# Layer 0 scan: the backward directions' chunk sums leave PSUM by ScalarE and are added to the kept sums by GpSimd

## Chip, cores and metric

One core of a Trainium2 chip runs the whole program. The metric is the device time of one execution in microseconds (us); lower is better.

## What is computed

The program is a network of four layers on an image batch of 4 x 48 x 48 x 128. The change touches the first layer alone, a selective scan over each image in four directions, cut here to what matters:

```python
# per image: d = 256 channels, L = 48*48 = 2304 positions, N = 16 states, K = 4 directions
x0 = xc.reshape(B, d, L)                       # rows first
x1 = transpose(xc).reshape(B, d, L)            # columns first
xs = stack([x0, x1, x0[..., ::-1], x1[..., ::-1]])
dt = softplus(dt_proj(x_proj(xs)))
def step(h, inp):                              # once a position
    dA = exp(dt_l[..., None] * A)
    h = h * dA + (dt_l * u_l)[..., None] * B_l[:, :, None, :]
    y = einsum('bkdn,bkn->bkd', h, C_l)        # sum over the 16 states
    return (h, y)
y = ys[:, 0] + ys[:, 2][..., ::-1]             # a direction and its reverse
y1 = ys[:, 1] + ys[:, 3][..., ::-1]
```

So the results of directions 2 and 3 (the backward ones) are added to those of directions 0 and 1.

## The kernel before, in words

Layer 0 (`layer0`) handles the four images one after the other. For each image a first block normalizes, projects and convolves, a second block holds the scan, and a third adds up, gates and projects the output. The change lies in the scan block.

**Chunks and steps.** A direction is cut into 6 chunks of 384 positions, so an image has 24 chunks (g = 0 to 23): chunks 0 to 5 are direction 0, 6 to 11 direction 1, 12 to 17 direction 2, 18 to 23 direction 3. A chunk has 16 steps, one for each state (n = s % 16), of 256 channels as two halves of 384 columns. Directions 1 and 3 read the image by columns, so with strides.

**One step through the engines.** `make_input` (TensorE) brings the scan's input into PSUM, as 12 matmul instructions (L396) or, in the 6 of 16 steps named in `TURNED`, as 6 (L394) after three ScalarE copies (L477). For the other ten VectorE makes a diagonal matrix first (L539, two steps ahead). `decays` (ScalarE, L487, two instructions) makes the exponentials two steps ahead. `scan` (VectorE, L562) runs the recurrence over both halves, reading decays from SBUF and the input from PSUM. GpSimd multiplies the states by C (L630, `hC`) and, right behind, `carry(s + 3)` copies two columns of end states (L619; L617 zeroes them in a direction's first chunk) which scan s + 3 waits for by `s_cr`. TensorE transposes the product into `y_ps` and adds it up there over the 16 steps (`sum_states`, 6 instructions, L407), three steps behind the scan.

**Once a chunk,** spread over the 16 slots of the chunk before, the next chunk is projected (`project`): rows on TensorE in slot 0 (L350), copied by ScalarE in slot 1 (L448), two softplus of three ScalarE instructions in slots 3 and 6 (L458, L460, L462) and VectorE (L532), and the delta product on GpSimd in slot 7 (`delta_u`, L602, two instructions of 384 columns).

**The sum of a chunk.** `y_ps` has 768 columns in one place of PSUM only, so before TensorE writes the first product of the next chunk into it, it waits for `s_ye`, which says that the last sum has been taken out. In the forward directions ScalarE copies it into `yT` in slot 3 of the next chunk (`keep_y`, L493), behind the first softplus. In the backward directions VectorE adds it to `yT` in slot 2 (`add_y`, L569), behind scan 2. The last one of an image comes at the end of the block.

**Order.** Each engine's instructions run in the order in which its function writes them. There is no planner; all waiting is by semaphores. TensorE's wait is the line

```python
if n == 0 and g:
    pe.wait_ge(s_ye, g)
```

Of the kernel before, what the change touches and what calls it, by code (L numbers as in the profile page):

```python
# [11 lines left out]
ALU = mybir.AluOpType  # L12
ACT = mybir.ActivationFunctionType
# [3 lines left out]
P = 128  # L17
# [45 lines left out]
DI, NS, RK, KD = 256, 16, 8, 4  # L63
RC = 384
NRC = L // RC
PW = WW + 2
NTE = 5
LB = RC // P
NCH = KD * NRC
# [7 lines left out]
def layer0(nc, x_in, w, x_out, c_rows):  # L77
    with ExitStack() as ctx:
        def sb(name, shape, dt=F32):
            return ctx.enter_context(nc.sbuf_tensor("l0_" + name, shape, dt))  # L80
# [25 lines left out]
        yT = sb("yT", [P, 2, L // P, DI])  # L106
# [3 lines left out]
        def cut(at, n):  # L110
            return arena[:, at:at + n]
# [12 lines left out]
        Cs = cut(26616, NCS * RC).rearrange("p (r l) -> p r l", r=NCS)  # L124
        low = cut(28920, 2 * RC).rearrange("p (r l) -> p r l", r=2)
        BT = sb("BT", [P, 2, LB, NS])

        gate = cut(0, 2 * L).rearrange("p (h l) -> p h l", h=2)
        sq = cut(4608, 4 * RC).rearrange("p (r h l) -> p r h l", r=2, h=2)
# [6 lines left out]
        with nc.Block() as block:  # L136
# [30 lines left out]
        scan_sem = Semaphores(nc, ctx, "l0s_")  # L167
# [2 lines left out]
            "dtu_made", "dtu_turned", "dtu_copied"))  # L170
        s_xT, s_dg, s_x2, s_exp, s_scan, s_hc, s_y, s_ye = (scan_sem(n) for n in (
            "input_turned", "B_diagonal", "input_made", "decay_made", "scanned", "hC_made", "y_summed", "y_kept"))
        s_nil, s_cr = scan_sem("nil_columns"), scan_sem("carried")
        s_cw = [scan_sem(f"C_rows_stored_{r}") for r in range(2)]
        s_cl = [scan_sem(f"C_laid_{r}") for r in range(NCS)]
        s_xr, s_st, s_z, s_sg, s_gt, s_mn, s_ce, s_sq, s_vr, s_ln, s_rs, s_sc, s_gy, s_o, s_res = (sem(n) for n in (
# [4 lines left out]
        with nc.Fori(0, NB) as b:  # L181
# [110 lines left out]
            with nc.Block() as block:  # L292

                def chunk(g):

                    k, j = g // NRC, g % NRC
                    col = (NRC - 1 - j) * RC if k >= 2 else j * RC
                    return k, slice(col, col + RC)
# [141 lines left out]
                @block.scalar  # L440
                def _(act):
                    act.preload_act_table_set("natural_log_exp_and_others")

                    def copy_rows(g):
                        act.wait_ge(s_rows, g + 1)
                        if g >= 2:
                            act.wait_ge(s_cw[g % 2], 16 * (g // 2))
                        act.activation(low[0:RK + 2 * NS, g % 2, :], ps[0:RK + 2 * NS, work:work + RC], ACT.Copy).then_inc(s_lo, 1)  # L448

                    def copy_B(g):  # L450
                        act.wait_ge(s_btp, g + 1)
                        act.activation(BT[:, g % 2].rearrange("p t n -> p (t n)"), ps[:, work + RC:work + RC + LB * NS],  # L452
                                       ACT.Copy).then_inc(s_bt, 1)

                    def softplus(g, h):
                        n = 2 * g + h
                        act.wait_ge(s_dtp, n + 1)
                        act.activation(soft[:, h, :], ps[:, work:work + RC], ACT.Abs).then_inc(s_sf, 1)  # L458
                        act.wait_ge(s_sf, 3 * n + 1)
                        act.activation(soft[:, h, :], soft[:, h, :], ACT.Exp, scale=-1.0).then_inc(s_sf, 1)  # L460
                        act.wait_ge(s_sf, 3 * n + 2)
                        act.activation(soft[:, h, :], soft[:, h, :], ACT.Ln, bias=1.0).then_inc(s_sf, 1)  # L462

                    def copy_dtu(g, part):
                        act.wait_ge(s_tp, 2 * g + part + 1)
                        t, m = ((0, 2), (2, 1))[part]
                        act.activation(dtuT[:, g % 2, t:t + m, :].rearrange("p t d -> p (t d)"), ps[:, work:work + m * DI],
                                       ACT.Copy).then_inc(s_tc, 1)

                    def turned_input(s):  # L470
                        n, g, i = s % NS, s // NS, rank[s]
                        act.wait_ge(s_bt, g + 1)
                        act.wait_ge(s_tc, 2 * g + 2)
                        if i >= 2:
                            act.wait_ge(s_x2, turned[i - 2] + 1)
                        for t in range(LB):
                            ins = act.activation(xT[:, i % 2, t, :], dtuT[:, g % 2, t, :], ACT.Copy, scale=BT[:, g % 2, t, n:n + 1])  # L477
                        ins.then_inc(s_xT, 1)

                    def decays(s):  # L480
                        n, g = s % NS, s // NS
                        if n == 0:
                            act.wait_ge(s_dt, 2 * g + 2)
                        if s >= NDC:
                            act.wait_ge(s_scan, s - NDC + 1)
                        for h in range(2):
                            act.activation(decay[:, s % NDC, half(h)], dtv[:, g % 2, h, :], ACT.Exp,  # L487
                                           scale=A[:, g // NRC, h, n:n + 1]).then_inc(s_exp, 1)

                    def keep_y(g):  # L490
                        act.wait_ge(s_y, NS * (g + 1))
                        k, cs = chunk(g)
                        act.activation(yT[:, k, cs.start // P:cs.stop // P, :], y_ps, ACT.Copy).then_inc(s_ye, 1)  # L493

                    def project(g, slot):
                        if slot == 1:
                            copy_rows(g)
                        elif slot == 3:
                            softplus(g, 0)
                        elif slot == 6:  # L500
                            softplus(g, 1)
                        elif slot == 9:
                            copy_B(g)
                        elif slot == 12:
                            copy_dtu(g, 0)
                        elif slot == 14:
                            copy_dtu(g, 1)

                    for slot in range(NS):
                        project(0, slot)  # L510
                    for s in range(3):
                        if s in rank and s % NS in TURNED:
                            turned_input(s)
                        if s < 2:
                            decays(s)
                    for s in range(NSTEP):
                        if s + 3 < NSTEP and (s + 3) % NS in TURNED:
                            turned_input(s + 3)
                        if s + 2 < NSTEP:
                            decays(s + 2)  # L520
                        if s // NS + 1 < NCH:
                            project(s // NS + 1, s % NS)
                        g = s // NS - 1
                        if s % NS == 3 and 0 <= g < 2 * NRC:
                            keep_y(g)

                @block.vector
                def _(dve):
# [33 lines left out]
                        dve.tensor_tensor_scan(hbuf[:, n, run], decay[:, s % NDC, run],  # L562
                                               x2_ps[s % 2][:, run], 0.0, ALU.mult, ALU.add).then_inc(s_scan, 1)

                    def add_y(g):
                        dve.wait_ge(s_y, NS * (g + 1))
                        k, cs = chunk(g)
                        own = yT[:, k - 2, cs.start // P:cs.stop // P, :]
                        dve.tensor_tensor(own, own, y_ps, ALU.add).then_inc(s_ye, 1)  # L569

                    def project(g, slot):
                        if slot == 4:
                            delta(g, 0)
# [9 lines left out]
                    for s in range(NSTEP):  # L583
                        if s + 2 < NSTEP and (s + 2) % NS not in TURNED:
                            diagonal(s + 2)
                        scan(s)
                        if s // NS + 1 < NCH:
                            project(s // NS + 1, s % NS)
                        g = s // NS - 1
                        if s % NS == 2 and g >= 2 * NRC:  # L590
                            add_y(g)
                    add_y(NCH - 1)

                @block.gpsimd
                def _(pool):
# [12 lines left out]
                    def carry(s):  # L608
# [10 lines left out]
                            ins = pool.tensor_copy(pair(decay[:, s % NDC, :], at), pair(hbuf[:, n, :], end))  # L619
                        ins.then_inc(s_cr, 1)  # L620

                    delta_u(0)
                    for s in range(3):
                        carry(s)
                    for s in range(NSTEP):
                        pool.wait_ge(s_scan, s + 1)
                        pool.wait_ge(s_cl[s % NCS], 16 * (s // NCS + 1))
                        if s >= NHC:
                            pool.wait_ge(s_y, s - NHC + 1)
                        pool.tensor_tensor(hC[:, s % NHC], halves(hbuf[:, s % NS, :]), Cs[:, s % NCS, :].unsqueeze(1).broadcast_to([P, 2, RC]),  # L630
                                           ALU.mult).then_inc(s_hc, 1)
                        if s + 3 < NSTEP:
                            carry(s + 3)
                        if s % NS == 7 and s // NS + 1 < NCH:
                            delta_u(s // NS + 1)

            scan_sem.clear()

# [2044 lines left out]
```

## Time and profile before

| | |
|---|---|
| median of 3 runs | 8045.21 us (8036.98 to 8050.74) |
| the profiled execution, own time | 8063.09 us |
| its span, first to last instruction | 8061.3 us |
| mean granted TensorE clock | 0.952 of full speed |
| busy: TensorE / VectorE / ScalarE / GpSimd | 7207 / 5978 / 4073 / 3649 us |
| layer 0, from the first scan's start to the last scan's | 100.6 to 3904.2 us |

The times in a timeline are microseconds from the span's start. A span of an instruction in it can reach over the next one's start by up to 0.1 us, since engines are pipelined, so the pace of a queue is read from start to start. The mark of a chunk is L448, the ScalarE copy of slot 1, which occurs once in each of the 96 chunks. The name l_arena covers nearly all working tiles of the layer, so the lines tell them apart.

### The profile page before, as it was taken

How to read it: one execution, taken by the hardware profiler on the slowest of the kernel's cores; microseconds unless marked ns; L12 is line 12 of the kernel's file. 1: busy time of each engine (PE TensorE's matmuls, PEld its weight loads, DVE VectorE, ACT ScalarE, POOL GpSimd, SP SyncE). 2: the span in 40 equal slices, each digit the busy share in tenths (PEclk: the TensorE clock that was granted, in tenths of full speed). 3: DMA queues.
4: the chain of work that ended last, by engine and by line, in shares of the span. 5: the costliest groups of instructions: out<-in, count | busy, mean ns of one | idle time of the engine just before them, and what ended most of it. 6: DMA issues, size and time to landing. Idle time of an engine off the chain costs nothing. (4 is left out here: it accounts for less than half of the span.)

```text
span 8061.3 us, 170699 instructions
## 1 busy us (share of the span) xinstructions
PE 7207.0 (89%) x62518; PEld 6199.1 (77%) x62522; DVE 5978.0 (74%) x9091; ACT 4073.4 (51%) x8517; POOL 3649.1 (45%) x4036
## 2 busy tenths in 40 slices
PE   7999889998999989999756788879897999999999
PEld 6888668886788867888546666635666989989899
DVE  7999879997899978999644555445556767767677
ACT  5888568885688757887312222124443222222222
POOL 4888558885688846888355545411000000000000
PEclk9999999999999999999878899889998999999999
DMA  2333223232233312333365555400003434434343
GB/s 62 91 93 93 72 62 92 92 90 68 68 90 94 92 58 76 92 93 89 103 177 169 163 158 144 118 6 3 1 0 95 128 115 124 124 115 123 116 124 111
DMA packets 590233, 762.33 MB, mean 95 GB/s; under 512 B 51687, under 2 KB 527880, under 8 KB 587569
## 3 DMA queue, kind: packets, MB, share of 16 engines
q1 hardware_dynamic: 537777, 584.54, 24.4%
q0 software_dynamic: 51840, 169.91, 7.4%
q8 instruction: 346, 5.67, 0.3%
q14 instruction: 270, 2.21, 0.1%
HBM read 720.59 MB, written 33.66 MB: 94 GB/s over the span
## 5 line engine op out<-in xcount | busy, mean ns | idle before, releaser
L630 POOL TENSOR_TENSOR l_arena<-l_arena 128x768 f32<-128x768 f32 x1536 | 2589.9, 1687 | 454.4 <-DVE l_arena L562 447.8
L562 DVE TENSOR_TENSOR_SCAN l_arena<-l_arena,psum 128x772 f32<-128x772 f32 x1536 | 2663.7, 1750 | 176.7 <-PE psum L394 72.6
L487 ACT ACTIVATE l_arena<-l_arena,l_A 128x384 f32<-128x384 f32 x3072 | 1642.5, 603 | 36.2 <-DVE l_arena L562 32.8
L396 PE MATMUL psum<-l_arena 128*128 128x128 f32 x11520 | 1498.6, 280 | 46.9 <-DVE l_arena L562 43.3
L396 PEld LDWEIGHTS psum<-l_arena 128*128 128x128 f32 x11520 | 1366.8, 192 | 170.7 <-issue 147.1
L407 PE MATMUL psum<-l_ident,l_arena 128*128 128x128 f32 x9216 | 1257.5, 273 | 50.5 <-ACT l_yT L493 41.6
L407 PEld LDWEIGHTS psum<-l_ident,l_arena 128*128 128x128 f32 x9216 | 1055.2, 141 | 60.2 <-POOL l_arena L630 60.2
L2256 POOL TENSOR_TENSOR st_mab<-st_xr 128x384 f32<-128x384 f32 x8 | 7.9, 1003 | 2055.8 <-DVE st_xr L2246 2055.8
L1189 POOL DMA_INDIRECT l_G<-neighbours,l_idx x648 | 617.3, 953 | 677.1 <-PE psum L1237 324.9
L477 ACT ACTIVATE l_arena<-l_arena,l_BT 128x256 f32<-128x256 f32 x1728 | 746.7, 496 | 7.5
L2531 ACT ACTIVATE st_own_s<-psum 128x384 f32<-128x384 f32 x256 | 125.5, 490 | 1089.9 <-PE psum L2368 1089.9
L1237 PE MATMUL psum<-l_ident,l_G 128*128 128x128 f32 x2592 | 363.8, 303 | 175.0 <-ACT l_val L1362 139.0
L2368 PE MATMUL psum<-st_FS,st_xt 128*128 128x128 f16 x6912 | 518.0, 219 | 2.0 <-DMA st_FS<-filter_sums 2.0
L539 DVE TENSOR_TENSOR l_arena<-psum,l_BT 128x384 f32<-128x384 f32 x960 | 510.2, 532 | 3.3 <-ACT l_BT L452 3.3
L1237 PEld LDWEIGHTS psum<-l_ident,l_G 128*128 128x128 f32 x2592 | 337.2, 158 | 205.4 <-issue 199.7
L394 PEld LDWEIGHTS psum<-l_ident,l_arena 128*128 128x128 f32 x3456 | 380.4, 140 | 143.8 <-issue 141.3
L394 PE MATMUL psum<-l_ident,l_arena 128*128 128x128 f32 x3456 | 486.9, 277 | 2.8 <-DVE l_arena L562 2.8
L2388 PE MATMUL psum<-st_Uc,st_Wm 128*128 128x128 f32 (+1 forms) x2560 | 448.6, 306 | 6.4 <-DVE st_Uc L2508 6.4
L2368 PEld LDWEIGHTS psum<-st_FS,st_xt 128*128 128x128 f16 x6912 | 434.7, 97 | 18.7 <-DMA st_FS<-filter_sums 2.4
L1032 DVE TENSOR_TENSOR l_G<-l_G,psum 128x1536 f32<-128x1536 f32 (+1 forms) x144 | 365.5, 2547 | 84.9 <-DMA l_G<-neighbours,l_idx 73.5
L2358 PE MATMUL psum<-st_F,st_xt 128*128 128x128 f16 x4608 | 427.4, 219 | 0.0
L2388 PEld LDWEIGHTS psum<-st_Uc,st_Wm 128*128 128x128 f32 x2560 | 351.4, 191 | 7.6 <-DVE st_Uc L2508 7.6
(438 smaller groups left out, 11300.3 us busy)
## 6 DMA issues: line engine op xcount, KB each, us to landing
l_arena<-c_rows SPq DMA_DIRECT2D x1536, 192.0 KB, 3.0
st_FS<-filter_sums SPq DMA_DIRECT2D x128, 1155.0 KB, 9.3
st_F<-filter_parts SPq DMA_DIRECT2D x128, 320.5 KB, 7.1
neighbours<-l_xt SPq DMA_DIRECT2D x256, 72.0 KB
st_mab<-in_st_mp SPq DMA_DIRECT2D x68, 256.0 KB, 9.3
st_mab<-in_st_mm SPq DMA_DIRECT2D x68, 256.0 KB, 6.1
l_G<-neighbours,l_idx POOLq DMA_INDIRECT x648
l_gnx<-in_x SPq DMA_DIRECT2D x4, 1152.0 KB, 5.5
```

The lines of the kernel that those rows point to most:

```text
L394: mm = pe.transpose(ps[:, o:o + P], xT[:, rank[s] % 2, t, h * P:(h + 1) * P], ident[:])
L396: mm = pe.matmul(ps[:, o:o + P], dtuT[:, g % 2, t, h * P:(h + 1) * P], diagB[:, rank[s] % 3, t, :], start=True, stop=True)
L407: mm = pe.matmul(y_ps[:, t, h * P:(h + 1) * P], hC[:, s % NHC, h, t * P:(t + 1) * P], ident[:], start=(n == 0 and h == 0 and t % 2 == 0), ...
L477: ins = act.activation(xT[:, i % 2, t, :], dtuT[:, g % 2, t, :], ACT.Copy, scale=BT[:, g % 2, t, n:n + 1])
L487: act.activation(decay[:, s % NDC, half(h)], dtv[:, g % 2, h, :], ACT.Exp, scale=A[:, g // NRC, h, n:n + 1]).then_inc(s_exp, 1)
L539: dve.tensor_tensor(diagB[:, i % 3], ident_ps.unsqueeze(1).broadcast_to([P, LB, P]), BT[:, g % 2, :, n:n + 1].broadcast_to([P, LB, P]), AL ...
L562: dve.tensor_tensor_scan(hbuf[:, n, run], decay[:, s % NDC, run], x2_ps[s % 2][:, run], 0.0, ALU.mult, ALU.add).then_inc(s_scan, 1)
L630: pool.tensor_tensor(hC[:, s % NHC], halves(hbuf[:, s % NS, :]), Cs[:, s % NCS, :].unsqueeze(1).broadcast_to([P, 2, RC]), ALU.mult).then_i ...
L1189: pool.indirect_dma_start(out=G[:, g, 4 * k:4 * k + 4, :].rearrange("p q c -> p (q c)"), out_offset=None, in_=tables[b], in_offset=bass.In ...
L1237: mm = pe.matmul(bank(i % 2, P * a, P * (a + 1)), G[:, g, 4 * k + q, :], ident[:], start=(q == 0), stop=(q == 3), is_transpose=True, skip_ ...
L2368: mm = pe.matmul(ps[:, at + i * P:at + (i + 1) * P], xt[:, xpart, x0 + LB - 1 - i, :], FS[:, r, fpart, z, three, shift + i * P:shift + (i ...
L2388: mm = pe.matmul(ps[:, o:o + hi - lo], Wm[:, r, z, m, :], src[:, lo - c * RC:hi - c * RC], start=False, stop=False, skip_group_check=True)
```

## The change

The diff:

```diff
+        ykeep = sb("ykeep", [P, 2, LB, DI])
...
-        s_nil, s_cr = scan_sem("nil_columns"), scan_sem("carried")
+        s_nil, s_cr, s_ya = scan_sem("nil_columns"), scan_sem("carried"), scan_sem("y_added")
...
                     def keep_y(g):
                         act.wait_ge(s_y, NS * (g + 1))
                         k, cs = chunk(g)
-                        act.activation(yT[:, k, cs.start // P:cs.stop // P, :], y_ps, ACT.Copy).then_inc(s_ye, 1)
+                        if g >= 2 * NRC + 2:
+                            act.wait_ge(s_ya, g - 2 * NRC - 1)
+                        dst = yT[:, k, cs.start // P:cs.stop // P, :] if k < 2 else ykeep[:, g % 2]
+                        act.activation(dst, y_ps, ACT.Copy).then_inc(s_ye, 1)
...
-                        if s % NS == 3 and 0 <= g < 2 * NRC:
+                        if s % NS == 3 and g >= 0:
                             keep_y(g)
+                    keep_y(NCH - 1)
...
-                    def add_y(g):
-                        dve.wait_ge(s_y, NS * (g + 1))
-                        k, cs = chunk(g)
-                        own = yT[:, k - 2, cs.start // P:cs.stop // P, :]
-                        dve.tensor_tensor(own, own, y_ps, ALU.add).then_inc(s_ye, 1)
...
-                        g = s // NS - 1
-                        if s % NS == 2 and g >= 2 * NRC:
-                            add_y(g)
-                    add_y(NCH - 1)
...
+                    def add_y(g):
+                        pool.wait_ge(s_ye, g + 1)
+                        k, cs = chunk(g)
+                        own = yT[:, k - 2, cs.start // P:cs.stop // P, :]
+                        pool.tensor_tensor(own, own, ykeep[:, g % 2], ALU.add).then_inc(s_ya, 1)
...
                         if s % NS == 7 and s // NS + 1 < NCH:
                             delta_u(s // NS + 1)
+                        if s % NS == 5 and s // NS > 2 * NRC:
+                            add_y(s // NS - 1)
+                    add_y(NCH - 1)
```

In all four directions ScalarE now takes the chunk's sum out of PSUM in slot 3 of the next chunk; in the backward ones it goes to one of two buffers of the new tile `ykeep`. GpSimd adds it to the kept sums in slot 5. ScalarE waits for the addition of two chunks before (`s_ya`) before it overwrites a buffer.

How the instructions stand now. GpSimd, in chunk 13, from the product and carry of slot 4 on; L631 is the product (L630 before), L614 the carry's copy (L619 before) and L597 the delta product (L602 before):

```order
L631 TENSOR_TENSOR l_arena<-l_arena 128x768
L614 COPY l_arena<-l_arena 128x2
L631 TENSOR_TENSOR l_arena<-l_arena 128x768
L614 COPY l_arena<-l_arena 128x2
L621 TENSOR_TENSOR l_yT<-l_yT,l_ykeep 128x768
L631 TENSOR_TENSOR l_arena<-l_arena 128x768
L614 COPY l_arena<-l_arena 128x2
L631 TENSOR_TENSOR l_arena<-l_arena 128x768
L614 COPY l_arena<-l_arena 128x2
L597 TENSOR_TENSOR l_arena<-l_arena,l_xc 128x384 x2
L631 TENSOR_TENSOR l_arena<-l_arena 128x768
L614 COPY l_arena<-l_arena 128x2
```

The row L621 is new: it stands behind product and carry of slot 5 and two slots ahead of the delta product. The rest of the queue is as before.

VectorE before the change, in chunk 13, from the last diagonal product and scan of slot 1 on:

```order
L539 TENSOR_TENSOR l_arena<-psum,l_BT 128x384
L562 SCALAR_TENSOR_TENSOR l_arena<-l_arena,psum 128x772
L569 TENSOR_TENSOR l_yT<-l_yT,psum 128x768
L562 SCALAR_TENSOR_TENSOR l_arena<-l_arena,psum 128x772
L539 TENSOR_TENSOR l_arena<-psum,l_BT 128x384
```

The row L569 is gone now, and scan 3 follows scan 2 directly.

ScalarE in chunk 13 with the change, slots 1 to 4; L459, L461 and L463 are the softplus (L458, L460, L462 before):

```order
L449 ACTIVATE l_arena<-psum 40x384
L478 ACTIVATE l_arena<-l_arena,l_BT 128x256 x3
L488 ACTIVATE l_arena<-l_arena,l_A 128x384 x4
L459 ACTIVATE l_arena<-psum 128x384
L461 ACTIVATE l_arena<-l_arena 128x384
L463 ACTIVATE l_arena<-l_arena 128x384
L497 ACTIVATE l_ykeep<-psum 128x768
L478 ACTIVATE l_arena<-l_arena,l_BT 128x256 x3
```

The row L497 is new here; in the forward directions it stood in the same place before, as L493.

## Rows read from the trace of the kernel before

**Rows 1.** The page, costliest groups: busy us, mean ns | idle before, its releaser.
```profile
L630 POOL TENSOR_TENSOR l_arena<-l_arena 128x768 f32<-128x768 f32 x1536 | 2589.9, 1687 | 454.4 <-DVE l_arena L562 447.8
L562 DVE TENSOR_TENSOR_SCAN l_arena<-l_arena,psum 128x772 f32<-128x772 f32 x1536 | 2663.7, 1750 | 176.7 <-PE psum L394 72.6
```

**Rows 2.** Lines L493 and L569: duration ns; who waited for L493; what L569 waited for.
```profile
L493 ACT ACTIVATE l_yT<-psum x48: 791/792/792, 142.6 to 3497.4; 128x768 f32<-128x768 f32 x48
...
  PE psum L407: 41.6, 44
```
```profile
L569 DVE TENSOR_TENSOR l_yT<-l_yT,psum x48: 953/954/955, 560.4 to 3908.6; 128x768 f32<-128x768 f32 x48
...
  PE psum L407: 41.0, 48
```

**Rows 3.** Line L448 in four stretches, directions 0, 1, 2, 3: first and last start.
```profile
L448 ACT ACTIVATE l_arena<-psum x4: 483/484/484, 136.8 to 239.8; 40x384 f32<-40x384 f32 x4
...
L448 ACT ACTIVATE l_arena<-psum x4: 483/484/484, 239.8 to 346.6; 40x384 f32<-40x384 f32 x4
...
L448 ACT ACTIVATE l_arena<-psum x4: 483/484/485, 557.0 to 660.1; 40x384 f32<-40x384 f32 x4
...
L448 ACT ACTIVATE l_arena<-psum x6: 483/483/485, 660.1 to 838.4; 40x384 f32<-40x384 f32 x6
```

**Rows 4.** VectorE's timeline, a backward chunk (direction 3): start, us, instruction [idle before, releaser].
```profile
770.54 0.95 DVE L569 TENSOR_TENSOR l_yT<-l_yT,psum 128x768 f32<-128x768 f32 x1 [0.72 <-PE psum L407]
...
803.70 1.76 DVE L562 TENSOR_TENSOR_SCAN l_arena<-l_arena,psum 128x772 f32<-128x772 f32 x1 [1.84 <-POOL l_arena L619]
```

**Rows 5.** VectorE's timeline, a forward chunk (direction 1): scans 4, 6 and 11.
```profile
424.11 1.76 DVE L562 TENSOR_TENSOR_SCAN l_arena<-l_arena,psum 128x772 f32<-128x772 f32 x1 [0.81 <-PE psum L396]
...
428.69 1.75 DVE L562 TENSOR_TENSOR_SCAN l_arena<-l_arena,psum 128x772 f32<-128x772 f32 x1
...
438.87 1.75 DVE L562 TENSOR_TENSOR_SCAN l_arena<-l_arena,psum 128x772 f32<-128x772 f32 x1
```

**Rows 6.** GpSimd's timeline, same chunk: carry 8, products 6, 7, 8, carry 11, product 9.
```profile
430.02 0.19 POOL L619 COPY l_arena<-l_arena 128x2 f32<-128x2 f32 x1
430.52 1.68 POOL L630 TENSOR_TENSOR l_arena<-l_arena 128x768 f32<-128x768 f32 x1 [0.31 <-DVE l_arena L562]
...
432.69 1.69 POOL L630 TENSOR_TENSOR l_arena<-l_arena 128x768 f32<-128x768 f32 x1 [0.37 <-DVE l_arena L562]
...
436.79 1.69 POOL L630 TENSOR_TENSOR l_arena<-l_arena 128x768 f32<-128x768 f32 x1
438.42 0.19 POOL L619 COPY l_arena<-l_arena 128x2 f32<-128x2 f32 x1
438.56 1.70 POOL L630 TENSOR_TENSOR l_arena<-l_arena 128x768 f32<-128x768 f32 x1
```

**Rows 7.** Timelines in a chunk of direction 0: carry 8, product 7, carry 11; scan 11.
```profile
217.39 0.18 POOL L619 COPY l_arena<-l_arena 128x2 f32<-128x2 f32 x1
...
220.06 1.69 POOL L630 TENSOR_TENSOR l_arena<-l_arena 128x768 f32<-128x768 f32 x1 [0.37 <-DVE l_arena L562]
...
225.37 0.21 POOL L619 COPY l_arena<-l_arena 128x2 f32<-128x2 f32 x1
```
```profile
226.23 1.75 DVE L562 TENSOR_TENSOR_SCAN l_arena<-l_arena,psum 128x772 f32<-128x772 f32 x1
```

**Rows 8.** GpSimd's groups by form, two-input additions and subtractions: busy us, mean ns | idle.
```profile
L1785 POOL TENSOR_TENSOR mo_ep<-mo_ep 128x512 f32<-128x512 f32 x36 | 49.3, 1369 | 243.3 <-DVE mo_ep L1771 243.3
...
L2260 POOL TENSOR_TENSOR st_mab<-st_xr 128x256 f32<-128x256 f32 x12 | 8.4, 723 | 0.0
...
L2256 POOL TENSOR_TENSOR st_mab<-st_xr 128x384 f32<-128x384 f32 x8 | 7.9, 1003 | 2055.8 <-DVE st_xr L2246 2055.8
```

**Rows 9.** VectorE's timeline, additions in an image's last chunk and at its end.
```profile
911.06 0.95 DVE L569 TENSOR_TENSOR l_yT<-l_yT,psum 128x768 f32<-128x768 f32 x1 [0.30 <-PE psum L407]
...
939.42 0.95 DVE L569 TENSOR_TENSOR l_yT<-l_yT,psum 128x768 f32<-128x768 f32 x1 [2.73 <-PE psum L407]
```

## The prediction

> **What bounds the kernel now.** I first read the page's costliest groups, to see which engines the touched loop loads. Its three large groups off TensorE are GpSimd's product of states and C (L630, 1687 ns), VectorE's scan (L562, 1750 ns) [rows 1] and the ScalarE exponentials. No engine is full over the whole chunk, so shares say little, and the question is what each chunk waits for. I write "scan(n)" for step n of the 16 of a chunk, "product(n)" for L630 of that step, and "carry(n)" for the small GpSimd copy (L619) that scan(n) needs and that GpSimd makes right behind product(n-3).
>
> Second, the two ways in which a chunk's sum leaves PSUM now, line by line [rows 2]. In the forward directions the ScalarE copy (L493, 792 ns, 48 times) makes TensorE wait 41.6 us over 44 chunks, 0.95 us each. In the backward directions the VectorE addition (L569, 954 ns, 48 times) makes nobody wait, but VectorE itself waits for it 41.0 us, 0.85 us each.
>
> Third, the pace of chunks, from the first and last start of L448, which comes once a chunk [rows 3]. Direction 0 takes (239.8 - 136.8) / 3 = 34.33 us, direction 2 (660.1 - 557.0) / 3 = 34.37; direction 1 takes (346.6 - 239.8) / 3 = 35.60, direction 3 (838.4 - 660.1) / 5 = 35.66. This is the heart of the matter: the forward half already is what the change makes of the backward half, apart from GpSimd's addition, and it is only 0.04 and 0.06 us a chunk quicker.
>
> The engines' own timelines say why. In a backward chunk VectorE waits 0.72 us for TensorE, adds, and then never stops until the next chunk's stall of 1.84 us [rows 4]. In a forward chunk it has no addition, but TensorE, held by ScalarE, delivers late: scan(4) idles 0.81 us [rows 5], and smaller idles around it eat the rest. From there on both halves run alike.
>
> **What the change removes and adds.** Removed: 48 VectorE additions, with their waits. Added: 48 ScalarE copies out of PSUM and 48 GpSimd additions of 128x768 f32, all SBUF. ScalarE copies at slot 3, behind the three softplus pieces, exactly as in the forward half. Priced by the forward pace, removal and copy together give -0.04 us in a chunk of direction 2 and -0.06 in one of direction 3. The 0.87 us of VectorE work do not come back as time, since the wait of TensorE for ScalarE takes their place.
>
> **The GpSimd addition.** It comes in slot 5, behind product(5) and carry(8), and two steps ahead of the delta product of slot 7 (L602). No row shows a 768-element GpSimd addition. The nearest by size is the product, 1687 ns [rows 1]; but one input of that is broadcast over the two halves. Additions and subtractions of two full inputs take 723 ns for 256, 1003 for 384 and 1369 for 512 elements [rows 8]. The first two rise by 0.28 us per 128, so 768 gives 1.003 + 3 x 0.28 = 1.84 on a straight line, and 1.369 + 2 x 0.28 = 1.93 from the third, which is the upper end; the product, 1.69, is the lower. I take 1.80 us, just under the straight line, since the product shows that a long instruction can cost less per element. What it takes in the queue is 0.04 to 0.06 us less than its duration (product and carry together take 438.56 - 436.79 = 1.77 us, the carry 438.56 - 438.42 = 0.14 of it, so 1.63 for a product of 1.69 [rows 6]): 1.76, between 1.63 and 1.88. The Trainium skill, "GPSIMD Engine Reference", section 4.1 on engine selection, speaks against such a move: elementwise work of two inputs belongs on VectorE, GpSimd being about twice as slow. Section 3.1 there has 4497 ns for a 2048-element f32 addition; in proportion that is an estimate of 1.69 us for 768, and the sum below would be that of its low end.
>
> Is it hidden? On average yes: 16 x 1.77 for products and carries, 436.79 - 432.69 - 1.77 = 2.33 for the delta product [rows 6] and 1.76 for the addition are 32.4 us, and a chunk has 35.6. Locally no. I follow the queue in a chunk of direction 1 [rows 6]. Carry(8) starts at 430.02, the addition would start at 430.16 and end its slot at 431.92, where product(6) now starts at 430.52. Product(7) follows 1.77 later, at 433.69 in place of 432.69: the short idles (0.31 and 0.37 us) are used up, and 1.00 us is left. From product(7) on GpSimd already runs without a gap, through the delta product, product(8) (436.79) and carry(11) (438.42), so carry(11) comes 1.00 us late. Scan(11) is at 438.87 [rows 5]; carry(11) ends at 438.42 + 0.19, and with a handover of 0.10 (a scan of 428.69 + 1.75 = 430.44 lets its product start at 430.52, 0.08 later) there is a slack of 0.16. **Scan(11) is thus 0.84 us late.** Scans 9 and 10 have their carries in time, being made ahead of the long delta product. Carry(12) follows carry(11) by 1.77, and scan(12) follows scan(11) by a scan of 1.75 and the diagonal product that lies between the two, so it does not wait; over the later steps too GpSimd's 1.77 a step is the quicker pace. Nothing more is added, but nothing is caught up either, since VectorE has no idle until the next chunk's stall, and that stall hangs on scan(15) through TensorE.
>
> In directions 0 and 2 the delta product reads straight rows and is shorter. The same steps [rows 7]: carry(8) at 217.39, so the addition would start at 217.53 and product(7) at 221.06 in place of 220.06, 1.00 late again; the slack at scan(11) is 226.23 - (225.37 + 0.21 + 0.10) = 0.55, so scan(11) is 0.45 us late.
>
> **The sum.** Additions with a delta product behind them stand in chunks 13 to 22 of each image. Chunks 13 to 16 prepare direction 2: 4 x (0.45 - 0.04) = 1.6 us. Chunks 17 to 22 prepare direction 3: 6 x (0.84 - 0.06) = 4.7 us. Chunk 23 has no projections and no delta product, so GpSimd has room; VectorE loses its addition and a wait of 0.30 [rows 9], 1.2 us, of which TensorE, waiting for ScalarE, should give back 0.1: -1.1 us. At the very end of the scan the last sum, now 0.95 us on VectorE [rows 9] and followed by nothing in the block, becomes 0.79 (copy) + 0.15 (one more handover) + 1.80: +1.8 us. Together 1.6 + 4.7 - 1.1 + 1.8 = 7.0 us an image, **28 us over four**. The profiled execution took 8063 us for a span of 8061; its own forecast is 8091. It is 18 above the median of the runs, 8045, and the difference carries over: 8045 + 28 = **8073 us**.
>
> The bounds of the addition change eleven places an image: at 1.63 each is 0.13 less, 22 us in all; at 1.88 it is 0.12 more, 33 us. If chunk 23 gives nothing back, 4 more, and handovers of 0.15 in place of 0.10 (the value taken at the end of the scan) add 2. With the spread of the runs (8037 to 8051, so 7 either way) the forecast's own range is 8060 to 8091.
>
> **The rivals.** (a) *Faster: VectorE is the bound and is relieved.* For it: in a backward chunk VectorE really has no idle from its addition on, and wait and addition are 0.72 + 0.87 = 1.59 us, 48 times 76 us, which would be 7969. Against it: the pace of the forward half, which has no such addition. It decides only if TensorE gets its bank back about 0.95 us sooner than in a forward chunk, that is if ScalarE copies ahead of the softplus, and its order has not changed. Chance 0.08. (b) *The addition is hidden.* GpSimd now idles 35.6 - 30.6 = 5 us a chunk. If scan(11) had a slack over 1.0 us, or the addition took under 1 us, only the ends would count: -0.5 (the forward pace over ten chunks) - 1.1 + 1.8, or 0.2 an image, 8046. Against it are the 0.16 and 0.55 of above, and the fixed order of the queue. Chance 0.12. (c) *The addition and the scan hinder each other,* a full addition for each of 48: 48 x 1.8 = 86 more, 8159. Against it: products run beside nearly every scan, and its mean is 1750 [rows 1]. Chance 0.03. (d) That the VectorE addition remains is excluded by the order of the instructions.
>
> **The numbers.** The forecast has 0.77. A measurement of this kernel tells a change from none from about 0.2%, 16 us, on. Nearly all of the forecast and (c) lie above that, a low end with a low measurement below: slower 0.77, same 0.15, faster 0.08. The range takes in (b) and the upper bound: 8046 to 8092, and leaves out (a), (c) and little of the rest.
>
> **What would show it.** Right: L448 spaced 34.8 us in direction 2 and 36.4 in direction 3, forward unchanged; the new addition 48 times at 1.80 us; the copy 96 times at 0.79 and TensorE waiting 0.95 for each backward one; and 40 waits of a scan for a GpSimd carry, behind the delta product, of 0.4 to 0.9 us. Wrong: a backward pace below 34.3 and 35.6 (rival a), equal to the forward one (b), or scans above 1.8 us (c). An addition near 1.69 would only move the size.

## The result, and the profile after

The changed kernel takes 8071.62 us (median of 13 runs, 8052.20 to 8095.02), the kernel before 8037.24 us in the same comparison (13 runs, 8032.84 to 8058.13). The ratio is 1.0037, with a 95% interval of 1.0028 to 1.0046: slower by about 30 us, where the prediction had 28.

The two profiled executions differ by less, 8080.4 against 8061.3 us of span. In layer 0 they differ by 32 us: the last GpSimd addition starts at 3940.0 and takes 1.8, the last VectorE addition of before started at 3908.6 and took 0.95 [rows 2]. Single executions also differ elsewhere, in layers that the change does not touch; here that took 13 us back.

The pace, from the first and last start of the once-a-chunk ScalarE copy, in directions 0, 1, 2 and 3, changed kernel:

```profile
L449 ACT ACTIVATE l_arena<-psum x4: 484/486/486, 136.3 to 239.3; 40x384 f32<-40x384 f32 x4
...
L449 ACT ACTIVATE l_arena<-psum x4: 484/484/486, 239.3 to 346.1; 40x384 f32<-40x384 f32 x4
...
L449 ACT ACTIVATE l_arena<-psum x4: 484/486/490, 556.5 to 661.0; 40x384 f32<-40x384 f32 x4
...
L449 ACT ACTIVATE l_arena<-psum x6: 483/483/487, 661.0 to 842.8; 40x384 f32<-40x384 f32 x6
```

That is 34.33 and 35.60 us forward, as in [rows 3], and (661.0 - 556.5) / 3 = 34.83 and (842.8 - 661.0) / 5 = 36.36 backward, where [rows 3] had 34.37 and 35.66. Two of the five last chunks took about 36.15 us and three 36.50; the part on the prediction comes back to them. All of the loss in pace lies in the backward directions.

The new GpSimd addition, and the ScalarE copies, of the changed kernel (duration ns least/median/most; below, who waited):

```profile
L621 POOL TENSOR_TENSOR l_yT<-l_yT,l_ykeep x48: 1799/1827/1837, 568.5 to 3940.0; 128x768 f32<-128x768 f32 x48
```
```profile
L497 ACT ACTIVATE l_ykeep<-psum x48: 791/792/812, 562.3 to 3939.1; 128x768 f32<-128x768 f32 x48
...
  PE psum L408: 79.5, 84
```

TensorE now waits 0.95 us for the copy in 84 chunks, where it was 44 [rows 2]: 40 more, with the new copies. What VectorE's scans wait for, before and then changed (us, times):

```profile
  PE psum L394: 72.6, 64
  PE psum L396: 49.4, 92
  POOL l_arena L619: 39.4, 24
  ACT l_arena L487: 13.5, 52
```
```profile
  PE psum L397: 89.1, 168
  POOL l_arena L614: 74.2, 64
  PE psum L395: 57.9, 56
  ACT l_arena L488: 26.2, 101
```

The waits put down to the GpSimd carry copy rise from 24 to 64. These sums must be taken apart by step. In the timelines scan(11) of each of the ten backward chunks with an addition and a delta product (13 to 22) now waits for its carry, in all four images, and before the change none did: 36 of these 40 waits are in the 64, and the four of chunk 18, whose carries are the zero fills, stand on the line L612. The other 28 of the 64 are the stall at scan(2), which was there before and which the profile puts down now to the carry, now to TensorE. That the difference of the two counts is 40 as well is chance. The waits for TensorE and ScalarE rise too, but they stand in place of the VectorE addition that is gone, as in the forward half.

A backward chunk (direction 3) of the changed kernel, VectorE's timeline, scans 3, 4 and 11:

```profile
772.78 1.76 DVE L567 TENSOR_TENSOR_SCAN l_arena<-l_arena,psum 128x772 f32<-128x772 f32 x1 [0.23 <-PE psum L397]
...
775.81 1.76 DVE L567 TENSOR_TENSOR_SCAN l_arena<-l_arena,psum 128x772 f32<-128x772 f32 x1 [0.82 <-PE psum L397]
...
791.46 1.76 DVE L567 TENSOR_TENSOR_SCAN l_arena<-l_arena,psum 128x772 f32<-128x772 f32 x1 [0.82 <-POOL l_arena L614]
```

And GpSimd's timeline of the same chunk: carry 8, the addition, product 6, and after the delta product, product 8 and carry 11:

```profile
781.72 0.19 POOL L614 COPY l_arena<-l_arena 128x2 f32<-128x2 f32 x1
781.86 1.82 POOL L621 TENSOR_TENSOR l_yT<-l_yT,l_ykeep 128x768 f32<-128x768 f32 x1
783.65 1.68 POOL L631 TENSOR_TENSOR l_arena<-l_arena 128x768 f32<-128x768 f32 x1
...
787.19 2.36 POOL L597 TENSOR_TENSOR l_arena<-l_arena,l_xc 128x384 f32<-128x384 f32 x2
789.52 1.68 POOL L631 TENSOR_TENSOR l_arena<-l_arena 128x768 f32<-128x768 f32 x1
791.15 0.18 POOL L614 COPY l_arena<-l_arena 128x2 f32<-128x2 f32 x1
```

The idles of 0.31 and 0.37 us in [rows 6] are gone, nothing in this queue stands still from carry 8 to carry 11, and scan(11) starts 0.13 us after carry(11) has ended (791.15 + 0.18 = 791.33, 791.46).

### The profile page after: what moved, and what is told of

It is laid out like the page before. It is cut to its first block and busy times, and to the rows that moved or that the text cites. A ratio compares the mean times of both kernels' runs of the same rounds, so it can differ in the third digit from the quotient of the medians.

```text
span 8080.4 us, 170795 instructions
## 1 busy us (share of the span) xinstructions
PE 7208.7 (89%) x62522; PEld 6195.4 (77%) x62522; DVE 5948.1 (74%) x9043; ACT 4103.3 (51%) x8565; POOL 3728.2 (46%) x4084
## 5 line engine op out<-in xcount | busy, mean ns | idle before, releaser
L567 DVE TENSOR_TENSOR_SCAN l_arena<-l_arena,psum 128x772 f32<-128x772 f32 x1536 | 2664.7, 1751 | 252.6 <-PE psum L397 89.1
L631 POOL TENSOR_TENSOR l_arena<-l_arena 128x768 f32<-128x768 f32 x1536 | 2594.1, 1690 | 404.1 <-DVE l_arena L567 400.6
L1193 POOL DMA_INDIRECT l_G<-neighbours,l_idx x648 | 617.5, 953 | 659.3 <-PE psum L1241 312.9
```

What stands on the lines that cost most here:

```text
L1193: pool.indirect_dma_start(out=G[:, g, 4 * k:4 * k + 4, :].rearrange("p q c -> p (q c)"), out_offset=None, in_=tables[b], in_offset=bass.In ...
```

## The experiments

The eleven runs were made later, on two chips of the same kind: changed_again, early_forward and early_slot5 on one, the other eight on the other. The kernel before takes 7771.76 us on the first and 7774.47 or 7775.89 on the second; each difference is taken to the kernel before of the same session. The theories have the loss in different places. G: only the place of the GpSimd addition costs, by making carry(11) late. Its rivals: S, the ScalarE copy with TensorE's wait costs; T, GpSimd's extra work costs wherever it stands; V, VectorE's relief is worth 1.59 us a chunk and is only covered up.

**The changed kernel again (changed_again).**

> The changed kernel once more, on the chip of the other runs, for comparison. About 30 us above the kernel before, pace 34.85 and 36.5 us.

7804.13 against 7771.76 us, ratio 1.0040 (1.0026 to 1.0053): the 30 us are there too, with the same pace.

**One part at a time: the ScalarE copy without the addition (copy_alone).**

```diff
-                        if g >= 2 * NRC + 2:
-                            act.wait_ge(s_ya, g - 2 * NRC - 1)
...
-                        if s % NS == 5 and s // NS > 2 * NRC:
-                            add_y(s // NS - 1)
-                    add_y(NCH - 1)
```

> The changed kernel without the 48 GpSimd additions (the backward sums are copied out by ScalarE but not added to the kept ones). Theory G: the forward pace, 34.33 and 35.60 us, in the backward directions, and total 4 to 8 us below the kernel before (10 chunks x 0.05 and 1.1 us in the last chunk of each image). Rival S: pace 34.85 and 36.5, total about 30 above. Rival V (VectorE is the bound and its relief is worth 1.59 us a chunk, only hidden by the addition): pace 32.8 and 34.1, total 76 below.

7768.78 against 7775.89, 7 us below, ratio 0.9991 (0.9982 to 1.0000). The backward pace, directions 2 and 3:

```profile
L449 ACT ACTIVATE l_arena<-psum x4: 484/484/492, 557.3 to 660.5; 40x384 f32<-40x384 f32 x4
...
L449 ACT ACTIVATE l_arena<-psum x6: 484/484/487, 660.5 to 838.5; 40x384 f32<-40x384 f32 x6
```

In direction 3 it is 35.60 us. In direction 2 two of the three chunks take 34.34 and one 34.56, as the changed kernel's forward half too has one longer chunk in each image (35.9 us); why is not known. S and V are both out: the copy costs nothing against the VectorE addition, and earns next to nothing.

**The other part: the addition without the copy (addition_alone).** The kernel before, with the tile `ykeep`, which VectorE zeroes once at the start, and with this line in GpSimd's loop:

```diff
+                        if s % NS == 5 and s // NS > 2 * NRC:
+                            pool.tensor_tensor(ykeep[:, 0], ykeep[:, 0], ykeep[:, 1], ALU.add)
```

> The kernel before (VectorE adds out of PSUM) with one extra 768-element GpSimd addition on a tile of its own in slot 5 of the backward chunks 13 to 23. Theory G: scan(11) late by as much as in the changed kernel, pace 34.85 and 36.5 us, last chunk and end of the image unchanged, total 24 to 28 us above the kernel before. Rival S: pace 34.4 and 35.65 as before, total unchanged.

7805.84 against 7775.89, 30 us above, ratio 1.0038 (1.0024 to 1.0052). The added instruction (1828 ns) takes the whole loss by itself; the total is a little above the 24 to 28 expected. The pace was 34.95 and mostly 36.62, 0.1 above the changed kernel's: in the kernel before, scan(5) of a backward chunk starts 11.35 us after the row projection, in a forward chunk 11.23, and the queue of GpSimd follows it; that this is the reason is argued, not tried.

**What VectorE's relief is worth at most (nothing_taken).** The kernel before, with the backward sums left in PSUM:

```diff
-                            pe.wait_ge(s_ye, g)
+                            pe.wait_ge(s_ye, min(g, 2 * NRC))
...
-                        if s % NS == 2 and g >= 2 * NRC:
-                            add_y(g)
-                    add_y(NCH - 1)
```

> The kernel before with the backward sums not taken out of PSUM at all (no VectorE addition, no copy, TensorE does not wait for its bank in the backward directions; their sums are left out of the output). It is what all relief of VectorE could be worth. Theory G: scan(4) still waits about 0.8 us for TensorE, which is busy without a gap from the row projection on; only the 0.24 us before scan(5) and 0.05 elsewhere go, so pace 34.1 and 35.35 us, and with 1.2 + 1 us at the end of each image a total 15 to 25 us below. Rival V: pace 32.8 and 34.1, total 76 below.

7749.57 against 7775.89, 26 us below, ratio 0.9965 (0.9952 to 0.9979). The backward pace, directions 2 and 3:

```profile
L448 ACT ACTIVATE l_arena<-psum x4: 483/484/485, 557.3 to 659.1; 40x384 f32<-40x384 f32 x4
...
L448 ACT ACTIVATE l_arena<-psum x6: 483/484/485, 659.1 to 835.1; 40x384 f32<-40x384 f32 x6
```

It is 33.93 and 35.20 us: of the 1.59 us a chunk that VectorE spends on and around its addition, 0.44 come back, a little more than the 0.3 expected. The rest is TensorE's, which works without a gap from the row projection to scan(4)'s input; scan(4) waits 0.82 us for it here too, with nothing that holds TensorE up. V is out for good.

**The place of the addition: slots 3, 9 and 13.** Each (slot3, slot9, slot13) is the changed kernel with one number changed:

```diff
-                        if s % NS == 5 and s // NS > 2 * NRC:
+                        if s % NS == 3 and s // NS > 2 * NRC:
```

> The addition on GpSimd moved from slot 5 to slot 3, behind product(3) and carry(6). Theory G (the addition costs time only where it makes carry(11) late): in the changed kernel's chunk of direction 3 carry(6) starts at 776.25 and product(4) at 777.65, after 1.21 us idle, and product(5) at 780.10, after 0.63 idle. The addition (1.79 us in the queue) would run from 776.6 to 778.4, product(4) comes 0.7 late and product(5) 0.1, so nothing is late from slot 6 on: pace 34.3 us in direction 2 and 35.6 in direction 3, and only the end of each image is longer, total within 5 us of the kernel before. Rival T (GpSimd's work counts wherever it stands) and rival S (the ScalarE copy and TensorE's wait for it are what costs): pace 34.85 and 36.5 as in the changed kernel, total about 30 us above the kernel before.

7776.76 against 7775.89, ratio 0.9997 (0.9988 to 1.0006). The loss is gone with the same work on the same engines. GpSimd's timeline in a chunk of direction 3, from carry 6 to product 5 and then product 6:

```profile
771.25 0.19 POOL L614 COPY l_arena<-l_arena 128x2 f32<-128x2 f32 x1
771.49 1.84 POOL L621 TENSOR_TENSOR l_yT<-l_yT,l_ykeep 128x768 f32<-128x768 f32 x1
773.30 1.68 POOL L631 TENSOR_TENSOR l_arena<-l_arena 128x768 f32<-128x768 f32 x1
774.92 0.19 POOL L614 COPY l_arena<-l_arena 128x2 f32<-128x2 f32 x1
775.11 1.68 POOL L631 TENSOR_TENSOR l_arena<-l_arena 128x768 f32<-128x768 f32 x1
776.73 0.19 POOL L614 COPY l_arena<-l_arena 128x2 f32<-128x2 f32 x1
777.22 1.69 POOL L631 TENSOR_TENSOR l_arena<-l_arena 128x768 f32<-128x768 f32 x1 [0.31 <-DVE l_arena L567]
```

By product(6) GpSimd waits for VectorE again, 0.31 us as in [rows 6]: the addition has gone into the idle of slots 4 and 5.

> The GpSimd addition in slot 9, behind product(9) and carry(12), after the delta product, where GpSimd still runs without a gap. Theory G: product(10) and with it carry(13) come 1.79 us late; against the rows before that is scan(13) late by 1.0 us in direction 2 and 1.4 us in direction 3: pace 35.3 and 37.0 us, total 45 to 55 us above the kernel before. Rival T: pace 34.85 and 36.5 as in the changed kernel, total 30 above.

7825.18 against 7774.47, 51 us above, ratio 1.0066 (1.0051 to 1.0082), pace 35.37 and 37.04. Scan(13) now waits 0.93 us in direction 2 and 1.33 in direction 3 (one of them, from VectorE's timeline):

```profile
873.93 1.76 DVE L567 TENSOR_TENSOR_SCAN l_arena<-l_arena,psum 128x772 f32<-128x772 f32 x1 [1.36 <-POOL l_arena L614]
```

T is out: with the same instruction in slot 9, 5 or 3 the changed kernel is 51, 32 or 1 us above the kernel before, and which carry comes late, and by how much, follows from the place.

> The addition in slot 13, behind product(13) and carry(0) of the next chunk. Theory G: carry(1) of the next chunk is at most 0.5 us late, and scan(1) is followed by a stall of scan(2) on the row projection, which takes that in: pace 34.33 and 35.60 us, total within 6 us of the kernel before. Rival T: pace 34.85 and 36.5, total 30 above.

7787.58 against 7774.47, 13 us above, ratio 1.0016 (1.0006 to 1.0025), a miss in the total. The pace was as expected, 34.34 and 35.60. What I had left out is the image's last chunk, which has no row projection and so no stall behind it. GpSimd's timeline at the end of an image there, the carry behind product 12, product 13, the addition, products 14 and 15 and the last addition:

```profile
932.43 0.19 POOL L614 COPY l_arena<-l_arena 128x2 f32<-128x2 f32 x1
932.57 1.68 POOL L631 TENSOR_TENSOR l_arena<-l_arena 128x768 f32<-128x768 f32 x1
934.21 1.83 POOL L621 TENSOR_TENSOR l_yT<-l_yT,l_ykeep 128x768 f32<-128x768 f32 x1
935.98 3.31 POOL L631 TENSOR_TENSOR l_arena<-l_arena 128x768 f32<-128x768 f32 x2
941.15 1.80 POOL L621 TENSOR_TENSOR l_yT<-l_yT,l_ykeep 128x768 f32<-128x768 f32 x1 [1.85 <-ACT l_ykeep L497]
```

The addition stands right ahead of the last two products, on the path that ends the image. From the last once-a-chunk copy (874.24) to TensorE's last sum (939.35) it is 65.1 us here and 63.1 with slot 3: 2.0 us an image, so 8 of the 12 us between the two runs. The other 4 are less than the intervals, 7 us to each side, can tell.

**The place of the ScalarE copy (early_copy).** The copy in slot 2, ahead of the softplus, in all directions, and the addition in slot 3:

```diff
-                        if s % NS == 3 and g >= 0:
+                        if s % NS == 2 and g >= 0:
                             keep_y(g)
...
-                        if s % NS == 5 and s // NS > 2 * NRC:
+                        if s % NS == 3 and s // NS > 2 * NRC:
```

> In all directions ScalarE copies the chunk's sum in slot 2, ahead of the softplus, and GpSimd adds in slot 3. The run without any taking out had a pace of 33.94 and 35.20 us in the backward directions; if TensorE's 0.95 us wait for the copy is all that stands between 34.33 and that, the copy ahead of the softplus (ScalarE idles 0.59 us before it) gives 33.95 to 34.05 and 35.2 to 35.3 in all four directions: 0.3 to 0.4 us in each of 92 chunks, less 0.7 us at each image's end, total 28 to 36 us below the kernel before. Rival: the delayed softplus delays the delta of slot 4 and takes as much back, total unchanged.

7737.58 against 7774.47, 37 us below, ratio 0.9954 (0.9940 to 0.9968), pace 33.94 and 35.20 in all four directions, which is that of nothing taken out at all. It beats both kernels. VectorE's timeline, scans 3, 4 and 5 in a chunk of direction 3, shows the wait of scan(5) (0.24 us in the changed kernel) gone and that of scan(4) left:

```profile
762.61 1.76 DVE L567 TENSOR_TENSOR_SCAN l_arena<-l_arena,psum 128x772 f32<-128x772 f32 x1 [0.23 <-PE psum L397]
...
765.64 1.76 DVE L567 TENSOR_TENSOR_SCAN l_arena<-l_arena,psum 128x772 f32<-128x772 f32 x1 [0.81 <-PE psum L397]
...
767.77 1.75 DVE L567 TENSOR_TENSOR_SCAN l_arena<-l_arena,psum 128x772 f32<-128x772 f32 x1
```

TensorE waits for no copy any more in this run, 0 times against 84.

**The same with the last sum added by VectorE (early_copy_last_dve).** ScalarE's and GpSimd's last instructions are taken out, and behind VectorE's loop stands:

```diff
+                    dve.wait_ge(s_y, NS * NCH)
+                    k, cs = chunk(NCH - 1)
+                    own = yT[:, k - 2, cs.start // P:cs.stop // P, :]
+                    dve.tensor_tensor(own, own, y_ps, ALU.add).then_inc(s_ye, 1)
```

> As early_copy, and the last sum of an image is added by VectorE straight out of PSUM, as in the kernel before. The end of an image is 1.7 us shorter than with copy and GpSimd addition: about 7 us below early_copy, 35 to 42 below the kernel before.

7736.65 against 7774.47, ratio 0.9953 (0.9939 to 0.9967). The 7 us did not show between the two medians; the intervals, 11 us to each side, could not have shown them for sure. In the first image TensorE's next block starts 4.4 us after the last sum in place of 6.1. Whether the gain is lost later, to a transfer, stays open.

**The early copy in the forward directions alone (early_forward).** The kernel before with `s % NS == 2` for `keep_y`.

> The kernel before with only the forward ScalarE copies moved from slot 3 to slot 2, ahead of the softplus; the backward additions stay on VectorE. If the gain of early_copy comes from the copy's place, chunks 1 to 12 gain 0.40 us each: pace 33.94 and 35.20 us in the forward directions, 34.38 and 35.65 in the backward ones, total 17 to 20 us below the kernel before; early_copy's other 18 us are then what ScalarE and GpSimd are worth in the backward directions once both stand at the right place.

7752.70 against 7771.76, 19 us below, ratio 0.9975 (0.9965 to 0.9986). So of the 37 us half belong to the forward directions, where nothing else was changed, and the other 18 are what moving the backward sums off VectorE is worth when both new instructions stand well (the two ratios, 0.9975 and 0.9954, were taken on different chips and lie 0.0021 apart, with intervals of 0.0010 and 0.0014 to each side, which just overlap; the pace, 34.38 and 35.65 against 33.94 and 35.20 backward, says it more sharply).

**The early copy with the addition left in slot 5 (early_slot5).**

> The changed kernel with the copy in slot 2 in all directions and the addition left in slot 5. Theory G: the scans of a backward chunk run 0.4 us earlier, the queue of GpSimd from slot 5 on follows them, so carry(11) is again late by its 0.9 us at most: backward pace 34.45 to 34.5 and 36.1, forward 33.94 and 35.20, total 5 to 15 us below the kernel before. If the addition's place did not matter, it would be as early_copy, 37 below.

7768.20 against 7771.76, ratio 0.9995 (0.9986 to 1.0004), 4 us below, just under the expected span. The backward pace is 34.53 and 36.17, scan(11) waiting 0.87 us for its carry: an earlier copy doesn't cure the place of the addition, and the gain it makes is spent there.

## Why the prediction was right

**The bound.** That the forward half shows what the backward half would be was the main step, and but for the one chunk of 34.56 it held to 0.01 us a chunk: copy_alone has 34.34 and 35.60 where the forward half has 34.33 and 35.60. The 0.87 us of VectorE work did not come back.

The reason that the prediction gave for this is wrong in part. It said that TensorE, held by ScalarE, brings scan(4)'s input late. TensorE's timeline in a chunk of direction 3 of the changed kernel, scan(4)'s input, the first product of the new chunk's sum behind its wait for the copy, and scan(5)'s input:

```profile
774.00 1.60 PE L397 MATMUL psum<-l_arena 128*128 128x128 f32 x12
776.55 0.85 PE L408 MATMUL psum<-l_ident,l_arena 128*128 128x128 f32 x6 [0.95 <-ACT l_ykeep L497]
777.24 0.82 PE L395 MATMUL psum<-l_ident,l_arena 128*128 128x128 f32 x6
```

Scan(4) starts at 775.81, ahead of the end of that wait. Its 0.82 us are there in nothing_taken and early_copy as well, where TensorE waits for no copy: they are TensorE's own work. The wait for the copy makes scan(5)'s input late instead. The profile puts scan(5)'s 0.24 us down to ScalarE's exponentials, but those of step 5 had ended 4.7 us before, at 773.52, while its input ends at 778.06 and it starts at 778.26. From scan(4) to scan(5) it is 2.45 us with the wait and 2.13 in early_copy without it, and the whole wait is worth 0.40 us a chunk (34.34 against 33.94). The forecast did not suffer, since it took the forward pace as measured; the price of rival (a) did.

**The GpSimd addition.** Taken as 1.80 us, measured 1.827 (1.799 to 1.837); in the queue 1.79 where 1.76 was taken. The lower bound from the product, 1.69, was too low. So was the estimate of 1.69 in proportion to the figure of the Trainium skill ("GPSIMD Engine Reference", section 3.1). By the low end the total would have been 22. That GpSimd is about twice as slow as VectorE holds here: 1827 ns against 954, 1.9 times, though VectorE's addition had one input in PSUM. The straight line through the smaller subtractions [rows 8] gave 1.84 and was the better guide.

**Scan(11).** Predicted 0.84 late in a chunk of direction 3, it waited 0.82, and its start came 3.00 us after scan(10)'s where copy_alone has 2.10, so 0.90 late; chunk by chunk the pace there was 36.50 (36.44 by the prediction), and 34.85 (34.78) in direction 2. The chunk whose mark lies behind direction 3's first row projection took 36.13 against 35.65 before, still with the smaller delay, 0.48. In the first chunk of direction 3 it was 36.16 only: there the carries are the shorter zero fills (about 0.1 us against 0.19), which gives GpSimd some slack, and scan(11) waited 0.47. The prediction had not counted that; that the longer addition made up for it is luck.

**The last chunk and the end.** In copy_alone, from the last once-a-chunk copy to the last sum, 63.14 us against 64.19: 1.05 gained, 1.1 predicted. From there to the next block's first matmul 6.14 us in the changed kernel (943.36 to 949.50) and 4.30 before (938.51 to 942.81): 1.84 lost, 1.8 predicted.

**The sum.** 28 predicted, 30 by the ratio and 34 between the medians. Along the first image the changed kernel loses 5.5 us in chunks 13 to 21, gains 0.16 from the last once-a-chunk copy (in chunk 22) to the last sum, and loses 1.84 behind it: 7.2 us, 29 over four, where the prediction had 7.0. That the absolute 8073 lies within 2 us of the measured 8071.62 is luck: the 8045 it starts from, a median of three, was 8 above that of the thirteen. The 40 waits of scan(11) for a carry are there, of 0.4 to 0.8 us but for 0.2 in chunk 14. Rival (a), 76 us faster, failed at the condition it was given: TensorE does not get its bank back sooner. And its price was wrong: even where TensorE gets the bank at once (nothing_taken) only 26 us are there, since TensorE makes scan(4) wait on its own account, which the prediction had put down to ScalarE. Rival (b), the addition hidden, is wrong for slot 5 and comes true in slot 3, where the addition stands ahead of a wait. Rival (c) is out: the scan's mean is 1751 ns with the additions beside it, 1750 before.

## What to carry to other kernels

In a queue that runs in order, extra work costs what is left of it after the idles and the slack ahead of the next result that somebody waits for, not its share of the engine: with one 1.8 us instruction a chunk, on an engine with some 5 us of idle in each, this change came out at +51, +32, +13 or +1 us by its slot. Before work is moved onto an engine, find where that engine waits and where it catches up, put the work in front of a wait, and look at the last round apart, where no later stall takes a delay in. And if one half of a program already does what the change makes of the other, compare their paces first.

## What was not expected of the hardware

A GpSimd instruction of 128x768 f32 with two full inputs takes 1827 ns, while the product of the same size, one of whose inputs is broadcast over two halves, takes 1690; no run tells whether the broadcast or the operation makes the difference. And the same kernel differed by 3% between the first comparison and the later runs, 8037 and about 7775 us for the kernel before. The changed kernel has a trace of either, 8080.4 and 7798.3 us of span: the pace in the scan is the same, and the last scan starts at 3934.7 and 3929.0. The difference lies behind it: GpSimd's indirect transfers (L1193) run from 4085.1 to 5218.6 us in the one and from 4080.3 to 4949.9 in the other, which is 264 of the 282 us. Whether that is the chip or something else that differed is not shown.
